# Attention scores from two fp32r halves on quarters of the array, scored closer behind their maxima, with the sums fetched first in each step

## The chip, the cores and the metric

The kernel runs on one core of a Trainium2 chip. The metric is the device time of one execution in microseconds. Five engines work side by side, each through its own list of instructions in order: TensorE (PE) multiplies, VectorE (DVE), ScalarE (ACT) and GpSimd (POOL) work element by element, and SyncE (SP) issues DMAs. They wait for each other through semaphores. A stalled instruction stalls everything behind it on its engine.

## What is computed

A batch of 16 sequences of 512 tokens with 128 features goes through four layers, each with a residual: causal attention, a feed-forward block, rotary attention, and the same feed-forward block again. Both attentions have 16 heads of 8 features.

```python
x = x + attn_a(layernorm(x))   # causal, 3 heads with a reweighted softmax
x = x + ffn(layernorm(x))
x = x + attn_b(layernorm(x))   # rotary positions, no mask
x = x + ffn(layernorm(x))
# attention: q, k, v = x @ W + b
scores = einsum('bhqd,bhkd->bhqk', q, k) / sqrt(8)
out = einsum('bhqk,bhkd->bhqd', softmax(scores), v) @ Wo + bo
# ffn: h = silu(x w1) * (x w2); h = gelu(h h1); h = gelu(h h2); h w3
```

## The kernel before

Everything stays on the chip in `x`; only the stacks described below and the reciprocals of the denominators take a way through DRAM. Each attention stage is a software pipeline over 16 batch entries. In step `n`, batch `n+1` is normalised and projected to q, batch `n` gets its k and v, batch `n-1` gets the row maxima of its scores (`maxes` on PE, `max_of` on DVE), batch `n-2` gets its scores, exponentials (ACT) and weighted sums of v (`weigh` on PE), batch `n-3` has its sums fetched and its denominators inverted, and batch `n-4` is projected out. A step is cut into beats: 20 in the causal stage, 32 in the rotary one. The tables `CAUSAL_AT` and `ROTARY_AT` say in which beat each piece of other work stands, on each engine. In a beat PE multiplies one pair of score tiles for the maxima (M) and one for the scores proper (S), and one or two blocks of weighted sums (W), in the order MSWX or SMWX, X being the other work.

Scores need full precision. Before, q and k are each split on POOL into three bf16 parts (`high`, `middle_low`), SP stores the parts into `d_stack` in DRAM (`store`) so that six products lie under each other, and loads them back as stacks of 48 rows (`load`), one stack for each half of the array's 128 rows. Two more rows of `stack_q` hold the negated maxima in two bf16 parts (`aug`), so that the score product subtracts the maximum by itself. A q stack and a k stack are stored and loaded in every step with a batch.

SP is one list. In a step (`sync`) it issues, in this order: the q load of batch `n`, the x load, the maxima of heads in the second half of batch `n-2` (`aug` 1), the sums and denominators of batch `n-3` (`numerators`), the k store, the reciprocals, the k load, the reciprocals spread to 128 rows, the maxima of the first half of batch `n-1` (`aug` 0), and the q store of batch `n+1`. PE may not start the scores of a half before the `aug` of that half has landed:

```python
if i % (BEATS // 2) == 0:
    h = i // (BEATS // 2)
    pe.wait_ge(s[f"aug{h}"], count(32, b, 32))
```

The causal stage also masks the diagonal twice: for the maxima by small bf16 products of 64 rows (`mask_q`, `ident_s`) right behind each M, and for the exponentials on POOL (`mask`).

## Time and profile before

| | us |
|---|---|
| median of 3 runs | 2139.06 |
| lowest and highest | 2135.49, 2146.88 |
| the profiled execution, its own time | 2145.3 |
| the span of its profile | 2143.6 |

The causal stage takes from about 60 to 600 us of the span, the first feed-forward block to about 1000 us, the rotary stage to about 1740 us, and the second feed-forward block the rest. The rows are read by stage: a step is one trip of the pipeline, and its length is the number of microseconds in a window divided by the steps in it, counted by an instruction that stands a known number of times in each.

### The profile page before, as it was taken

The numbers are of one execution on the slowest core, as the hardware profiler recorded it, in microseconds if no ns is written. First come the engines' busy times: TensorE is split into PE (matmuls) and PEld (weight loads), VectorE is DVE, ScalarE is ACT, GpSimd is POOL, SyncE is SP. The second block draws the span as 40 slices with busy tenths as digits, with TensorE's granted clock in tenths as the row PEclk, the third lists the DMA queues.
The fourth block names the chain that finished last, engine by engine and source line by source line (L and its number), as shares of the span: only waits on it lengthen the run. The fifth ranks groups of instructions, "written<-read, shape, count | busy, mean of one in ns | idle before, by whom it ended". The sixth has DMA issues, their size and how long they took to land.

```text
span 2143.6 us, 43057 instructions
## 1 busy us (share of the span) xinstructions
PE 1941.3 (91%) x16196; PEld 980.7 (46%) x16196; DVE 1719.6 (80%) x2342; ACT 1481.3 (69%) x2641; POOL 1097.3 (51%) x1553
## 2 busy tenths in 40 slices
PE   3789998899879999997899999999999978999998
PEld 1333333334337777774222222222222226777776
DVE  4888887788738888875889999899998936888883
ACT  1477777677766666652588888888887875666665
POOL 5777777677445555564423333434333014555554
PEclk9799999899989999998799999999999999999999
DMA  7456665656210000004344443344444100000000
GB/s 176 95 117 127 118 128 108 111 110 124 49 24 29 1 1 1 1 7 82 61 82 92 92 87 72 72 91 88 92 87 87 33 13 12 15 11 15 11 15 16
DMA packets 106357, 136.71 MB, mean 64 GB/s; under 512 B 21153, under 2 KB 90018, under 8 KB 100002
## 3 DMA queue, kind: packets, MB, share of 16 engines
q1 hardware_dynamic: 106146, 133.89, 31.2%
q8 instruction: 133, 2.18, 0.5%
q14 instruction: 78, 0.64, 0.1%
HBM read 67.78 MB, written 55.58 MB: 58 GB/s over the span
## 4 chain that ended last, share of the span: by engine, by line
PE 48%; POOL 12%; SPq 10%; DMA 10%; issue 9%; DVE 7%; ACT 4%; POOLq 0%; ACTq 0%; DVEq 0%
PE ps_score L1451 20%; PE ps_out L1061 7%; PE ps_max L1451 5%; PE ps_score L1003 5%; SPq L580 4%; DMA o_num<-o_raw 4%; DVE negmax L872 4%; PE ps_max L1021 3%; DMA d_stack<-parts 3%; PE ps_out L1451 3%; ACT prob L989 2%; DMA stack_q<-nm_rows 2%; POOL xhat L322 2%; PE ps_max L1102 2%; SPq L558 2%
## 5 line engine op out<-in xcount | busy, mean ns | idle before, releaser
L989 ACT ACTIVATE prob<-ps_score 128x512 f32<-128x512 f32 x1664 | 899.1, 597 | 209.1 <-PE ps_score L1003 191.0
L872 DVE TENSOR_REDUCE negmax<-ps_max 128x2 f32<-128x1024 f32 (+1 forms) x896 | 907.4, 1064 | 141.0 <-PE ps_max L1038 84.7
L1061 PE MATMUL ps_out<-prob,v_aug 128*9 128x256 f32 (+2 forms) x6656 | 518.9, 392 | 27.4 <-ACT o_raw L952 24.0
L1451 PE MATMUL ps_score<-h,w_hi 128*128 128x512 f32 x2048 | 503.5, 399 | 9.4 <-POOL h L1225 8.3
L1451 PEld LDWEIGHTS ps_score<-h,w_hi 128*128 128x128 f32 x2048 | 383.6, 189 | 104.3 <-POOL h L1225 10.8
L1003 PE MATMUL ps_score<-stack_q,stack_k 50*128 50x512 bf16 (+3 forms) x2048 | 360.3, 353 | 58.0 <-ACT prob L989 38.8
L1021 PE MATMUL ps_max<-stack_k,stack_q 48*128 48x512 bf16 (+3 forms) x2048 | 344.7, 355 | 56.4 <-DVE negmax L872 32.6
L708 POOL TENSOR_SCALAR_AFFINE_SELECT prob<-prob 128x256 f32<-128x256 f32 (+1 forms) x448 | 188.1, 440 | 154.9 <-ACT prob L989 154.6
L1213 POOL TENSOR_TENSOR h<-h3f,h 128x512 fp32r<-128x512 f32 x128 | 192.0, 1508 | 134.0 <-ACT h L1363 134.0
L1003 PEld LDWEIGHTS ps_score<-stack_q,stack_k 50*128 50x128 bf16 x2048 | 105.4, 94 | 313.9 <-ACT prob L989 237.0
L1061 PEld LDWEIGHTS ps_out<-prob,v_aug 128*9 128x9 f32 x6656 | 106.2, 89 | 305.9 <-ACT prob L989 148.6
L1213 POOL TENSOR_TENSOR h<-h2f,h 128x512 fp32r<-128x512 f32 x128 | 172.6, 1350 | 66.7 <-ACT h L1363 66.7
L1021 PEld LDWEIGHTS ps_max<-stack_k,stack_q 48*128 48x128 bf16 x2048 | 87.7, 95 | 217.6 <-DVE negmax L872 103.6
L668 POOL TENSOR_TENSOR qf<-qf,turned 128x512 f32<-128x512 f32 x31 | 39.7, 1280 | 261.6 <-DVE turned L849 261.6
L1357 ACT ACTIVATE h3f<-ps_score,s_col 128x512 f32<-128x512 f32 x128 | 87.5, 684 | 112.3 <-PE ps_score L1451 108.2
L1357 ACT ACTIVATE h2f<-ps_score,s_col 128x512 f32<-128x512 f32 x128 | 88.1, 688 | 95.2 <-PE ps_score L1451 89.1
L1267 DVE CAST h<-h1f 128x512 fp32r<-128x512 f32 x120 | 124.8, 1040 | 35.0 <-PE ps_score L1451 33.9
L1451 PE MATMUL ps_max<-ffn_xT,w_hi 128*128 128x512 f32 x512 | 144.7, 415 | 3.2 <-DVE ffn_xT L1274 2.5
L332 DVE TENSOR_SCALAR xhat<-x,mv,rstd 128x128 f32<-128x128 f32 x128 | 95.1, 803 | 44.1 <-POOL rstd L304 44.1
L1254 DVE SCALAR_TENSOR_TENSOR ut<-tanh,ps_max 128x512 f32<-128x512 f32 x128 | 86.8, 678 | 54.2 <-ACT tanh L1374 51.6
L1269 DVE TENSOR_TENSOR h<-h1f,h 128x512 fp32r<-128x512 f32 x120 | 115.3, 961 | 4.1
L1102 PE MATMUL ps_max<-xT,weights 128*128 128x512 f32 x176 | 107.4, 694 | 4.0 <-ACT xT L933 3.0
(114 smaller groups left out, 2104.2 us busy)
## 6 DMA issues: line engine op xcount, KB each, us to landing
d_stack<-parts SPq DMA_DIRECT2D x128, 192.0 KB, 2.8
stack_q<-d_stack SPq DMA_DIRECT2D x64, 384.0 KB, 6.0
stack_k<-d_stack SPq DMA_DIRECT2D x64, 384.0 KB, 6.0
d_stack<-parts SPq DMA_DIRECT2D x128, 128.0 KB, 2.8
d_stack<-parts SPq DMA_DIRECT2D x128, 64.0 KB, 2.4
o_num<-o_raw SPq DMA_DIRECT2D x128, 64.0 KB
o_rden<-d_rden SPq DMA_DIRECT2D x128, 64.0 KB
x<-in_x SPq DMA_DIRECT2D x16, 256.0 KB, 6.9
```

The costliest lines, as they stand in the source:

```text
L708: last = pool.affine_select(out=tri, in_=tri, compare_op=ALU.is_ge, fill=0.0, base=0, pattern=[[0, tri.shape[1]], [1, P]], channel_multipl ...
L872: last = dve.tensor_reduce(m["negmax"][:, t, :, p], banks[:, :, at:at + w], AX.X, ALU.max, negate=True)
L989: act.activation(prob(b, i)[:, o], act_bank("score", 2 * i + o), ACT.Exp).then_inc(s["prob"], 1)
L1003: mm = pe.matmul(act_bank("score", 2 * i + o)[:, at:at + w], m["stack_k"][c][rows, p, P * j:P * (j + 1)], m["stack_q"][c][rows, p, S - w:S ...
L1021: last = pe.matmul(to[:, o, at:at + w], m["stack_q"][c][rows, p, P * t:P * (t + 1)], m["stack_k"][c][rows, p, 0:w], start=(piece == 0), st ...
L1061: last = pe.matmul(m["ps_out"][32 * g:32 * g + HD + 1, out:out + w], m["v_aug"][b % VALUES][:, j, 4 * G + g, :], prob(b, beat)[:, g % 2, l ...
L1102: pe.matmul(to, m["weights"][:, which], m["xT"][:], start=True, stop=True).then_inc(s[f"{name}_ps"], 1)
L1213: pool.tensor_tensor(h[k][:, 1, f], hf[k][:, f % 2], h[k][:, 0, f], ALU.subtract).then_inc(s[f"h{k}"], 1)
L1267: dve.tensor_copy(h[1][:, 0, f], h1f[:, f % 2]).then_inc(s["h1_hi"], 1)
L1269: dve.tensor_tensor(h[1][:, 1, f], h1f[:, f % 2], h[1][:, 0, f], ALU.subtract).then_inc(s["h1"], 1)
L1357: act.activation(hf[k][:, f % 2], m["ps_hid"][:, f % 2], ACT.Gelu, scale=m["s_col"][:, k, f:f + 1]).then_inc(s[f"h{k}f"], 1)
L1451: mm = pe.matmul(to, w[:, cols], moving(part), start=begin and i == 0, stop=last and i == len(pairs) - 1)
```

## The change

1. The q and k stacks are made of two fp32r parts and three products instead of three bf16 parts and six. POOL makes them with two instructions (`halves`) in place of four. A stack for a group of four heads now lies in a quarter of the array's rows: 24 rows from each multiple of 32, and the negated maximum in one more. `d_stack` is fp32 with the product index outside the quarter index. A load is four DMAs of 24 rows, a store is two DMAs of 128 rows.
2. The maxima need no split: PE transposes them in fp32, POOL's two instructions for them are gone, and `aug` is one DMA in place of two.
3. A pair `p` of heads lies in rows of quarters `2*(p%2)` and `2*(p%2)+1`, so a product pair takes two quarters, and M beats take the odd pair first. The mask products stay 64 rows high.
4. Scores, exponentials and sums of a batch stand `ahead` beats earlier: 4 in the causal and 7 in the rotary stage. Several slots in the tables move with them.
5. In a step SP issues the `numerators` first, ahead of the q load.
6. The flag of the weights' low part is moved in the last causal step.

```diff
-TERMS = 6
+TERMS = 3
 KROWS = TERMS * HD
-AUG = 2
+QUAD = P // 4
-LOADS = 2 * 16
+LOADS = 4 * 16
...
-CAUSAL_AT = {"k": 3, "nm1": 1, "v": 5, "proj": 8, "xT": 9, "nm0": 13, "q": 13, "weigh": (4, 5, 6, 7, 7), "out": 8,
+CAUSAL_AT = {"k": 3, "nm1": 2, "v": 5, "proj": 8, "xT": 9, "nm0": 12, "q": 13, "P_norm": 7, "P_v": 4, "P_bias": 11, "P_q1": 16, "P_k1": 4,
...
+             "D_proj": 9, "A_nm1": 3, "A_nm0": 13, "A_xT": 10, "order": "MSWX", "ahead": 4}
...
-    m["d_stack"] = dram("d_stack", (2, 2, 2, TERMS, HD, PAIRS, S), BF16)
+    m["d_stack"] = dram("d_stack", (2, 2, TERMS, 4, HD, GROUPS, S), F32)
...
     def aug(sp, h, b):
 
         sp.wait_ge(s[f"nm_row{h}"], b + 1)
-        for o in range(2):
-            at = SIDE * o + KROWS
-            sp.dma_start(m["stack_q"][b % STACKS][at:at + AUG, HALF * h:HALF * (h + 1), :],
-                         m["nm_rows"][2 * HALF * o:2 * HALF * (o + 1), h, :]).then_inc(s[f"aug{h}"], 16)
+        sp.dma_start(m["stack_q"][b % STACKS][KROWS::QUAD, GROUPS // 2 * h:GROUPS // 2 * (h + 1), :].bitcast(F32),
+                     m["nm_rows"][QUAD * h:QUAD * h + H // 2].bitcast(F32)).then_inc(s[f"aug{h}"], 16)
...
     def store(sp, b, name, i):
...
+        rows = m["d_stack"][b % 2, i].rearrange("t o d g n -> (o d g) t n")
+        parts = m["parts"][:, i].bitcast(F32)
+        if i == 0:
+            sp.dma_start(rows[:, 0:2], parts[:, 0:1].broadcast_to([P, 2, S])).then_inc(s[name], 16)
+            sp.dma_start(rows[:, 2:3], parts[:, 1:2]).then_inc(s[name], 16)
...
     def load(sp, b, name, stored, i):
...
-        for o in range(2):
-            rows = slice(SIDE * o, SIDE * o + KROWS)
-            sp.dma_start(m[name][b % STACKS][rows], m["d_stack"][b % 2, i, o].rearrange("t d p n -> (t d) p n"))\
-                .then_inc(s[name], 16)
+        for o in range(4):
+            rows = slice(QUAD * o, QUAD * o + KROWS)
+            sp.dma_start(m[name][b % STACKS][rows].bitcast(F32), m["d_stack"][b % 2, i, :, o]).then_inc(s[f"{name}{b % 2}"], 16)
...
     def sync(sp, n):
 
+        if on(n, 3):
+            numerators(sp, n - 3)
         if n == 0:
             store(sp, n, "stored_k", 1)
         if on(n, 0):
             load(sp, n, "stack_q", "stored_q", 0)
         if causal and on(n, -X_AHEAD):
             load_x(sp, m, a, n + X_AHEAD)
         if on(n, 2):
             aug(sp, 1, n - 2)
-        if on(n, 3):
-            numerators(sp, n - 3)
...
-    def high(pool, b, name, i):
+    def halves(eng, b, name, i):
...
+        eng.tensor_copy(m["parts"][:, i, 0], m["qf"][:, i]).then_inc(s["highs"], 1)
+        eng.wait_ge(s["highs"], count(2, b, i + 1))
+        wait(eng, s["parts"], count(2, b, i))
+        eng.tensor_tensor(m["parts"][:, i, 1], m["qf"][:, i], m["parts"][:, i, 0], ALU.subtract).then_inc(s["parts"], 1)
...
-    def scores(pe, n, i):
+    def scores(pe, n, b, i):
...
+                at_row = QUAD * (2 * (p % 2) + o)
+                rows = slice(at_row, at_row + KROWS + 1)
```

In the source of a load the three products lie 65,536 elements apart and the eight features of a product 2,048 apart, so the DMA reads it as 3 runs of 8 rows of 8 KB and writes it to 24 rows. Before, source and target were both plainly 48 rows.

SP's list in one causal step, before, from the q load on (sizes are partitions x elements of the target):

```order
L592 DMA stack_q<-d_stack 48x4096 [waits a_stored_q,a_score]
L592 DMA stack_q<-d_stack 48x4096
L548 DMA stack_q<-nm_rows 2x4x512 [waits a_nm_row1]
L548 DMA stack_q<-nm_rows 2x4x512
L555 DMA den<-o_raw 128x1x64 [waits a_rden,a_o_raw]
L558 DMA o_num<-o_raw 32x1x512 [waits a_oT]
```

and the same stretch of SP's list now, with the k load that follows it:

```order
L553 DMA den<-o_raw 128x1x64 [waits a_rden,a_o_raw]
L556 DMA o_num<-o_raw 32x1x512 [waits a_oT]
L556 DMA o_num<-o_raw 32x1x512 x3
L592 DMA stack_q<-d_stack 24x1x2048 [waits a_stored_q,a_score]
L592 DMA stack_q<-d_stack 24x1x2048 x3
L546 DMA stack_q<-nm_rows 4x2x512 [waits a_nm_row1]
L579 DMA d_stack<-parts 128x2x512 [waits a_parts]
L580 DMA d_stack<-parts 128x512
L561 DMA d_rden<-rden 128x64 [waits a_rden]
L592 DMA stack_k<-d_stack 24x1x2048 [waits a_stored_k,a_score]
L592 DMA stack_k<-d_stack 24x1x2048 x3
```

The sums (`o_num`) moved ahead of the q load, the q load became four DMAs, and the maxima row of the second half still stands right behind it.

PE's list in the causal stage where the second half of the scores begins, before:

```order
L1021 MATMUL ps_max<-stack_k,stack_q 128x128 [waits a_resid]
L1021 MATMUL ps_max<-stack_k,stack_q 128x128
L1021 MATMUL ps_max<-stack_k,stack_q 128x384 x2
L1038 MATMUL ps_max<-ident_s,mask_q 128x2x64 x4
L1003 MATMUL ps_score<-stack_q,stack_k 128x512 [waits a_prob,a_aug1]
L1003 MATMUL ps_score<-stack_q,stack_k 128x512 [waits a_prob]
```

and now:

```order
L979 MATMUL ps_max<-stack_k,stack_q 128x256 [waits a_k]
L979 MATMUL ps_max<-stack_k,stack_q 128x256 x3
L996 MATMUL ps_max<-ident_s,mask_q 128x2x64 x4
L1060 MATMUL ps_max<-weights,xT 128x128 [waits a_xT,a_max]
L1060 MATMUL ps_max<-weights,xT 128x128 x3
L960 MATMUL ps_score<-stack_q,stack_k 128x512 [waits a_prob,a_aug1]
L960 MATMUL ps_score<-stack_q,stack_k 128x512 [waits a_prob]
L979 MATMUL ps_max<-stack_k,stack_q 128x128 [waits a_max]
```

The wait for `aug1` stood in beat 10 of a causal step and stands in beat 6 now; in the rotary stage it moved from beat 16 to beat 9. That for `aug0` moved from beat 0 of the next step to beat 16 (causal) and 25 (rotary) of the step before.

## Rows read from the trace of the kernel before

**Rows 1.** Page, part 1: busy time and share of the span.

```profile
PE 1941.3 (91%) x16196; PEld 980.7 (46%) x16196; DVE 1719.6 (80%) x2342; ACT 1481.3 (69%) x2641; POOL 1097.3 (51%) x1553
```

**Rows 2.** Windows of causal and rotary stages: length, busy by engine, clock, DMA, GB/s.

```profile
100.00:550.00 450.00, 400.73 (x5218) 172.23 (x5212) 368.00 (x524) 330.65 (x626) 325.15 (x656) 0.95 0.61 118
...
1100.00:1600.00 500.00, 470.81 (x4568) 133.66 (x4570) 454.52 (x501) 418.56 (x785) 176.44 (x262) 1.00 0.42 83
```

**Rows 3.** Groups of instructions, causal window 100 to 550 us: busy, mean | idle before.

```profile
L868 DVE TENSOR_REDUCE negmax<-ps_max 128x4 f32<-128x1024 f32 x52 | 63.3, 1218 | 12.7 <-PE ps_max L1038 12.1
...
L708 POOL TENSOR_SCALAR_AFFINE_SELECT prob<-prob 128x256 f32<-128x256 f32 x313 | 121.5, 407 | 95.7 <-ACT prob L989 95.7
```

**Rows 4.** Chain of waits, causal stage: start, length, what.

```profile
302.10 0.42 SPq L592
...
305.41 0.68 SPq L548
306.13 3.88 DMA stack_q<-nm_rows
310.06 0.39 PE ps_score L1003 x2
...
390.53 11.65 DMA o_num<-o_raw
```

**Rows 5.** Timeline of SP, causal stage: start, length, DMAs issued.

```profile
315.86 0.78 SPq L592 DMA_DIRECT2D stack_q<-d_stack  x2
...
319.29 3.15 SPq L558 DMA_DIRECT2D o_num<-o_raw  x4
```

**Rows 6.** Windows of 1 us, columns as in rows 2; the last two are DMA.

```profile
1304.00:1305.00 1.00, 1.00 (x7) 0.32 (x3) 0.76 (x1) 0.87 (x2) 0.00 (x0) 1.00 0.96 206
...
1313.00:1314.00 1.00, 1.00 (x12) 0.14 (x12) 1.00 (x2) 0.95 (x3) 0.92 (x2) 1.00 0.44 161
...
1326.00:1327.00 1.00, 1.00 (x14) 0.26 (x12) 1.00 (x2) 0.74 (x2) 0.29 (x1) 1.00 0.96 172
...
1329.00:1330.00 1.00, 1.00 (x16) 0.28 (x12) 1.00 (x2) 1.00 (x3) 0.90 (x1) 1.00 0.54 131
```

**Rows 7.** Page, part 6: DMA issues, KB each, median us from issue to landing.

```profile
stack_q<-d_stack SPq DMA_DIRECT2D x64, 384.0 KB, 6.0
```

**Rows 8.** Timeline of PE in causal beats at either clock: start, length, instruction.

```profile
407.15 1.04 PE L1061 MATMUL ps_out<-prob,v_aug 128*9 128x256 f32 x8
...
415.35 0.62 PE L1061 MATMUL ps_out<-prob,v_aug 128*9 128x256 f32 x8
415.90 0.39 PE L1021 MATMUL ps_max<-stack_k,stack_q 48*128 48x512 bf16 x2
416.13 0.22 PE L1038 MATMUL ps_max<-ident_s,mask_q 64*128 64x64 bf16 x4
416.19 0.38 PE L1003 MATMUL ps_score<-stack_q,stack_k 50*128 50x512 bf16 x2
416.50 0.83 PE L1061 MATMUL ps_out<-prob,v_aug 128*9 128x384 f32 x8
```

**Rows 9.** Window behind a long causal stall, columns as in rows 2.

```profile
402.00:412.00 10.00, 8.58 (x87) 3.21 (x89) 4.20 (x5) 6.53 (x13) 3.87 (x8) 0.62 0.37 77
```

**Rows 10.** Waits in the rotary window 1100 to 1600 us: total, times, longest.

```profile
DVE negmax L872 <- PE ps_max L1021: 29.4, 46, 1.4
...
PE ps_out L1061 <- ACT o_raw L952: 18.7, 22, 1.7
```

**Rows 11.** Timeline of SP, rotary stage: start, length, DMAs issued.

```profile
1277.13 0.78 SPq L592 DMA_DIRECT2D stack_q<-d_stack  x2
...
1307.13 0.78 SPq L592 DMA_DIRECT2D stack_k<-d_stack  x2
...
1322.54 0.78 SPq L592 DMA_DIRECT2D stack_q<-d_stack  x2
```

More of the change, by code:

```diff
@@ L154, in buffers @@
         low("oT_pad", [P, S])
-        m["stack_q"] = [stack_q] + [low(f"stack_q{c}", [P, PAIRS, S], BF16) for c in range(1, STACKS)]
+        m["stack_q"] = [stack_q] + [low(f"stack_q{c}", [P, GROUPS, S], F32R) for c in range(1, STACKS)]
     h1, h2 = (sb(f"h{k}", [P, 2, FT, S], F32R) for k in (1, 2))
@@ L374, in __init__ @@
-        self.group = len(per_group)
-        self.beats = GROUPS * self.group
-        self.steps = B + 4
-        self.rotary = not causal
-        self.scores = [[(2 * G + half, j, at, w) for half, j, at, w in pieces] for G in range(GROUPS) for pieces in per_group]
-        self.diagonals = diagonals * GROUPS
-        self.maxes = [[(2 * G + half, t, at, w) for half, t, at, w in pieces] for G in range(GROUPS) for pieces in maxes]
-        self.weigh_at, self.reads, self.weighed = [], [], []
-        for G in range(GROUPS):
-            for at, beats, products in blocks:
-                self.weigh_at.append(self.group * G + at)
-                self.reads.append(self.group * G + beats[-1])
-                self.weighed.append((G, [(j, out, w, [(self.group * G + beat, lo) for beat, lo in where])
-                                         for j, out, w, where in products]))
@@ L395, in block_due @@
+        self.beats, self.blocks = len(self.scores), len(blocks)
+        self.weigh_at = [block[0] for block in blocks]
+        self.reads = [block[2] for block in blocks]
+        self.weighed = [(block[1], block[3:]) for block in blocks]
+        self.block_of = {beat: i for i, block in enumerate(blocks) for beat in block[6]}
     def block_due(self, i):
@@ L440, in attention @@
     for i in range(BEATS):
-        act_turns += [("score", 2, 2 * i + o) for o in range(2)]
+        step, at = ahead(0, i)
+        act_turns += [("score", 2 - step, 2 * at + o) for o in range(2)]
         dve_turns += [("max", 1, i)]
@@ L1042, in weigh @@
     def weigh(pe, b, k):
-        G, products = plan.weighed[k]
+        G, (j, out, w, beats, lo, start) = plan.weighed[k]
         first = k % (BLOCKS // GROUPS) == 0
```

303 lines of the change are left out of this document (134 added, 169 removed).

## The prediction

> **What bounds the kernel now.** I read the shares first, then the windows by stage, then the waits and the chain in each stage. No engine fills the span, PE comes nearest with 91% [rows 1], and the attention stages are where the change works.
>
> Causal stage: `L868` stands four times in a step and 52 times in 450 us [rows 3], so there were 13 steps of 34.6 us. PE was busy 400.73 us, 30.8 a step, and DVE 28.3 [rows 2]: nobody is full. The chain shows what is late. SP issues loads and stores one after another, and the small DMA with the maxima waits behind the k load and takes 3.88 us before PE may score; elsewhere ACT waits 11.65 us for `o_num`, queued the same way [rows 4]. The step is a loop through POOL, SP and the DMA queue.
>
> Rotary stage: a q load is issued at 1277.13 and at 1322.54 [rows 11], so a step is 45.4 us. DVE is busy 454.52 of 500 us, 41.3 a step, PE 42.8 [rows 2]. DVE sets the pace and loses 29.4 us in 500 to PE; PE loses 18.7 us to ACT's `o_raw` at the start of batches [rows 10]. At most 4.1 us a step are there to be won.
>
> **POOL and SP work.** Two of POOL's four split instructions per stack go and two copies and subtractions for maxima. POOL is busy 325.15 of 450 us in the causal stage [rows 2] and sits in its loop. SP's six store issues become two and the two of `aug` one, at 0.6 to 0.7 us each, against two loads more at 0.42 us [rows 4]. That would take some 4 us of issue time off the causal loop. It pays only if nothing else is late.
>
> **Sums first.** `o_num` no longer queues behind the q load, so the 11.65 us waits of the causal stage [rows 4] and the 18.7 us of the rotary one, 1.7 a step [rows 10], go. The price is that the q load is issued after them. In a causal step (t counts from PE's first beat) `o_num` waits for POOL's `weighted` of beat 1, about t = 3.9; its four issues take 3.15 us [rows 5]; the q load's issues start at 7.0 and its data at about 8.2.
>
> **PE.** M and S stay pairs of two products at a time, 512 columns in 0.23 us and S in 0.31 with what follows [rows 8]. In the causal stage M and S stand in different quarters, but four mask products of 64 rows lie between them; in the rotary stage both fall in the same half of the array (S is seven beats ahead and M starts with the odd pair), so nothing runs four wide in a beat. From M to mask, both on 64 rows, PE needs 0.23 us for 0.21 us of columns; from S to W, where the array is cut differently, 0.31 [rows 8]. So a new cut costs about 0.09 us. Going to the mask's 64 rows and back to 32 adds two in each causal beat: 20 x 2 x 0.09 = 3.6 us, and the fp32 transposes of the maxima 0.4. PE would have 34.8 us a causal step, 1.75 a beat. TensorEngine Tiling (Array Packing), section Key Properties, of the Trainium skill says that a change of tiling mode drains TensorE; by a reading in which the 32 and 64 row cuts count as one mode the 3.6 us would be 0. The trace before has no such change, so the bounds are 0 and 3.6 us, and I take 3.6, the price of the nearest one. Narrow products of 128 columns may cost more in fp32r: from nothing to 2.6 us a step, four times their columns (16 x 0.16 us). I take nothing and keep 2.6 for the range.
>
> **The load, on which I stake the forecast.** What a DMA spreads over follows the outermost size of its two sides. Stores with 64 rows on both sides fill 0.96 of the 16 DMA engines [rows 6] (the window from 1304). `o_rden` and `o_num` have 8 on their DRAM or source side and 32 on the other, and while four of them are queued the share stays at 0.44 and 0.54, that is, 7 to 9 engines [rows 6] (from 1313 and 1329). Four queued DMAs would fill 16 if each took other engines; they take the same eight. The new load has 3 outermost on one side and 24 on the other, so I expect three engines, and the four DMAs of a stack one behind another on the same three. The Trainium skill's DMA: Bandwidth & Descriptors, section "Why a DMA increments its semaphore by 16 and not by 1", says the same: the largest number up to 16 that divides both slowest dims, and on this path the lowest-numbered engines.
>
> A stack is still 786 KB: 262 KB for each of the three. Per engine the load before moved 172 / (16 x 0.96) = 11.2 GB/s, eight engines 161 / (16 x 0.44) = 22.9 GB/s [rows 6] (from 1326 and 1313). So the load occupies the three for L = 23.4 us or 11.4 us, where before it landed in 6.0 [rows 7]. I take 11.4: the rate per engine doubled where fewer worked.
>
> What stands behind it is the same `aug`, which now takes four engines, the three among them, and is needed sooner.
>
> - Causal: `aug` 1 lands at 8.2 + 11.4 + 2.5 (x load and its own landing) = 22.1. PE wants it in beat 6, t = 10.5. PE, and with it everyone, stands 11.6 us. 14 beats are left, 24.5 us, and PE comes back at a low clock: behind a stall like that the granted clock was 0.62 over 10 us [rows 9], its lower level of 1.2 GHz for much of it, and a W took 1.04 us in place of 0.62 [rows 8]; I put 2.5 us on it. Step: 49.1 us.
> - The other chain of the same step: the k store (48 KB an engine at 206 / (16 x 0.96) = 13.4 GB/s, 3.6 us [rows 6]) lands 4.8 us after `aug` 1, the k load starts 1 us later and takes 11.4, `o_rden` 1.4, `aug` 0 0.8. That is t = 41.5 for PE's beat 16, and 48.5 for the step. I take 49: 14.4 us more than 34.6.
> - Rotary: data from t = 5.7, `aug` 1 lands at 5.7 + 11.4 + 0.9 = 18.0. PE wants it in beat 9, at 1.42 us a beat t = 12.8. PE loses 5.2 us, which DVE feels but for a beat that it gets back as fewer waits of the old kind (1.5), against 1.5 for the clock. Step: 50.6, 5.2 more. `aug` 0 lands at about 39, before beat 25.
>
> The sum, against the profiled execution's 2145.3 us. 14 steps in each stage have a q load and a batch to score: 14 x 14.4 = 202 and 14 x 5.2 = 73. The first batch's two loads are longer by 7 us each with nothing to hide them in the causal stage, 14, and half hidden by the feed-forward block in the rotary one, 7. The stages' tails are 4 and 7 beats of exponentials shorter, 1.2 us each: -13. Total 2145.3 + 283 = 2428. The median stands 6 us under the profiled execution, so **about 2422 us**.
>
> **Rivals.**
> 1. *The load spreads over 16 engines after all* (each DMA on other engines, or cut otherwise). Then every wait above is gone and the step is PE's: causal 31.6 us without the 3.6, -42, rotary -21, tails -13: about 2065 us. With the 3.6 it is causal +8: about 2115. For it: the bytes are the same, the pieces of a store are 2 KB instead of 1. Against: the shares of four queued DMAs [rows 6]. It decides at L below 6 us, where `aug` 1 is in time again. Chance 0.10.
> 2. *Three engines, but at 11.2 GB/s each*, the rate of the old load. L = 23.4, and both stages follow the long chain: causal 18.8 + 2 L + 7 = 72.6 us, rotary 61.4 + 10 = 71.4. 14 x 38 + 14 x 26 + 57 - 13 = 940: about 3080 us. For it: that load read DRAM as this one does, `o_rden` reads it too but in little. Against: sixteen engines shared what three now have. Chance 0.08.
> 3. *Three engines, but most of the wait is covered*: SP runs ahead of my times, POOL's `weighted` comes earlier, or an engine moves more than 23 GB/s. At half the added wait 2290 us, at a quarter 2215; at less it is no change. Chance 0.10, of which 0.03 within 0.5%.
>
> **How the numbers follow.** The forecast has 0.72. L from 9 to 16 us, the cuts of the array at 0 or 3.6 us and the narrow products at 0 or 2.6 us a causal step give 2340 to 2640. With the third rival's greater part the range is 2250 to 2640: it leaves out the first rival, the second, and the far end of the third. A measurement of this kernel tells 0.5%, some 11 us, from no change. Faster 0.10 (rival 1), same 0.03, slower 0.87.
>
> **What would show it.** Right: in windows of a microsecond within a load the DMA share is near 3/16 = 0.19, and loads land in 10 us or more instead of 6; PE's longest waits are for `stack_q<-nm_rows`, some 10 us a causal step in beat 6, and the granted clock of the causal stage falls well under 0.95; the feed-forward stages are as before. Of the smaller steps: PE's time from M to the mask products grows from 0.23 to 0.32 us, and ACT no longer waits for `o_num` by 11 us. Wrong: a DMA share above 0.9 in a load. If the share is 0.19 and the steps are still short, my times of issue are wrong; if the loads take over 16 us, the rate per engine is.

## The result and the profile after

| | before | after |
|---|---|---|
| median, us | 2139.96 | 2662.18 |
| lowest and highest | 2135.49, 2146.88 | 2626.93, 2683.82 |
| the profiled execution, its span | 2145.3, 2143.6 | 2664.05, 2662.3 |

The changed kernel takes 1.238 times as long (95% interval 1.226 to 1.251). The forecast was 2422 us, with a range of 2250 to 2640: the sign holds, the size doesn't.

The page of the changed kernel, busy time and share of the span, then PE's granted clock in 40 slices. It answers to [rows 1].

```profile
PE 2317.5 (87%) x16196; PEld 1185.9 (45%) x16196; DVE 1748.7 (66%) x2340; ACT 1493.6 (56%) x2641; POOL 972.5 (37%) x1297
...
PEclk6678888788767999996858685866768688799999
```

PE has as many instructions as before and is busy 376 us more. The clock is low in both attention stages (slices 1 to 13 and 19 to 35), and full in the feed-forward stages. As in [rows 2], the windows of both attention stages: length, busy by engine, clock, DMA, GB/s.

```profile
150.00:600.00 450.00, 328.12 (x3824) 150.36 (x3818) 273.75 (x385) 245.76 (x461) 204.80 (x409) 0.83 0.27 86
1350.00:1750.00 400.00, 379.76 (x2526) 131.77 (x2524) 264.27 (x276) 234.33 (x435) 73.35 (x96) 0.72 0.18 58
```

The causal stage waits (PE busy 73%). The rotary stage does not: PE is busy 95% of the time, at 0.72 of its clock. The same two windows, groups by line: the reductions of the maxima, of which four (L826) make a causal step and 32 (L830) a rotary one.

```profile
L826 DVE TENSOR_REDUCE negmax<-ps_max 128x4 f32<-128x1024 f32 x38 | 45.9, 1208 | 0.2
...
L830 DVE TENSOR_REDUCE negmax<-ps_max 128x2 f32<-128x1024 f32 x193 | 234.9, 1222 | 104.3 <-PE ps_max L979 103.9
```

38/4 = 9.5 causal steps in 450 us are 47.4 us each (34.6 before). 193/32 rotary steps in 400 us are 66.3 us each; the kernel before has this row with x279 in a window of 400 us inside the stage, 45.9 us.

The whole difference can be laid out by the first and the last product for maxima of each stage. PE's timeline has them at these times (start, length, instruction):

```profile
46.95 0.90 PE L979 MATMUL ps_max<-stack_k,stack_q 24*128 24x128 f32 x4 [19.47 <-issue]
...
790.13 0.50 PE L979 MATMUL ps_max<-stack_k,stack_q 24*128 24x512 f32 x2
...
1198.82 0.80 PE L979 MATMUL ps_max<-stack_k,stack_q 24*128 24x512 f32 x4 [8.20 <-DMA stack_k<-d_stack]
...
2239.34 0.41 PE L979 MATMUL ps_max<-stack_k,stack_q 24*128 24x512 f32 x2
```

In the kernel before the same four stand at 42.96, 582.80, 984.55 and 1722.79. So the causal stage grew from 539.8 to 743.2 us (**+203**), the rotary one from 738.2 to 1040.5 (**+302**), and fill, first feed-forward block and last block by 4 + 7 + 2. The table uses these two lengths for every kernel, each from its profiled execution. Those lie within 6 us of the medians, but for f3 (30 us longer) and e2 (27 us shorter).

| kernel | median, us | ratio to before, 95% | causal | rotary |
|---|---|---|---|---|
| before | 2139.96 | | 539.8 | 738.2 |
| changed | 2662.18 | 1.226 to 1.251 | 743.2 | 1040.5 |
| e1 loads on 8 engines | 2332.98 | 1.085 to 1.093 | 665.4 | 805.4 |
| e2 loads on 12 | 2338.50 | 1.084 to 1.102 | 648.6 | 802.3 |
| e3 before, loads on 3 | 2381.80 | 1.109 to 1.114 | 648.1 | 842.1 |
| e4 maxima before q load | 2443.11 | 1.139 to 1.147 | 746.2 | 811.1 |
| f1 bf16 | 2531.16 | 1.163 to 1.175 | 687.7 | 970.6 |
| f2 8 engines, SP's old order | 2601.56 | 1.207 to 1.223 | 657.6 | 1070.8 |
| f3 8 engines, maxima first | 2581.79 | 1.191 to 1.208 | 647.1 | 1090.8 |
| f4 before, sums first | 2123.44 | 0.986 to 0.994 | 527.4 | 730.1 |
| g1 fp32r on halves | 2491.46 | 1.159 to 1.167 | 731.9 | 888.5 |
| g2 bf16 on halves | 2424.14 | 1.128 to 1.136 | 697.2 | 856.2 |
| h1 8 engines; sums, maxima, load | 2253.92 | 1.049 to 1.056 | 592.7 | 803.3 |
| h2 before; sums, maxima, load | 2118.29 | 0.986 to 0.992 | 528.7 | 725.6 |
| i1 h1, bf16 | 2179.44 | 1.015 to 1.023 | 566.9 | 756.4 |
| i2 h1, fp32r on halves | 2222.06 | 1.036 to 1.044 | 566.6 | 798.8 |
| i3 h1, bf16 on halves | 2161.94 | 1.008 to 1.015 | 555.9 | 754.5 |

**The causal stage took the time that was forecast.** The chain of waits of the changed kernel in one causal step (start, length, what) is the one that the forecast wrote down; it answers to [rows 4].

```profile
315.37 1.25 POOL oT L679
316.64 0.71 SPq L556
...
320.00 0.73 SPq L592
...
323.64 11.31 DMA stack_q<-nm_rows
334.99 0.48 PE ps_score L960
```

POOL's product of beat 1, the four `o_num`, the q load, and then a small DMA that lands 11.31 us after its issue because it stands behind the load. PE's waits there, total, times, longest, in 150 to 600 us:

```profile
PE ps_score L960 <- DMA stack_q<-nm_rows: 105.1, 9, 12.5
...
ACT o_raw L908 <- DMA o_num<-o_raw: 14.0, 8, 2.1
```

105.1/9 = 11.7 us a step; the forecast had 11.6. ACT's long wait for `o_num` is gone, as it had said. And in a microsecond in the middle of a load the DMA share is near 3/16, against the 0.96 of a load before in [rows 6] (from 1326):

```profile
1338.00:1339.00 1.00, 1.00 (x16) 0.41 (x12) 1.00 (x2) 0.88 (x2) 0.97 (x1) 1.00 0.17 74
```

**The rotary stage did not.** PE's waits for the maxima in 1350 to 1750 us:

```profile
PE ps_score L960 <- DMA stack_q<-nm_rows: 14.3, 4, 3.8
```

That is 2.4 us a step, where the forecast had 5.2. The wait is shorter than forecast; what follows it is longer. PE's timeline at full clock, and behind a wait:

```profile
1301.14 0.50 PE L960 MATMUL ps_score<-stack_q,stack_k 25*128 25x512 f32 x2
1301.48 0.41 PE L979 MATMUL ps_max<-stack_k,stack_q 24*128 24x512 f32 x2
...
1302.36 0.52 PE L960 MATMUL ps_score<-stack_q,stack_k 25*128 25x512 f32 x2
...
1342.79 0.79 PE L960 MATMUL ps_score<-stack_q,stack_k 25*128 25x512 f32 x2 [3.50 <-DMA stack_q<-nm_rows]
...
1344.91 0.79 PE L960 MATMUL ps_score<-stack_q,stack_k 25*128 25x512 f32 x2
```

A beat takes 1.22 us at full clock and 2.12 us behind the wait of 3.50 us. Windows of 5 us, of which many are left out, show how long that lasts (the clock is the third number from the end):

```profile
1335.00:1340.00 5.00, 4.29 (x36) 1.28 (x34) 4.36 (x5) 3.26 (x6) 2.16 (x3) 1.00 0.21 87
1340.00:1345.00 5.00, 2.21 (x14) 0.72 (x14) 1.25 (x2) 1.08 (x2) 0.99 (x1) 0.60 0.52 193
1345.00:1350.00 5.00, 5.00 (x28) 1.65 (x28) 2.72 (x3) 2.17 (x4) 0.00 (x0) 0.50 0.16 59
...
1415.00:1420.00 5.00, 5.00 (x23) 1.59 (x19) 2.36 (x3) 1.16 (x3) 0.00 (x0) 0.55 0.00 0
1420.00:1425.00 5.00, 5.00 (x54) 1.75 (x56) 4.91 (x6) 4.38 (x9) 3.17 (x3) 1.00 0.13 50
```

For 75 us PE is busy nearly all the time, at 1.2 GHz, and then goes back to 2.4. Between 1300 and 1800 us there are five such stretches: 80, 50, 20, 80 and 50 us. The Trainium skill, TensorE: Matmul & The Clock Gate, section "Part 1: The HAM clock gate", has PE at full clock again after a short time of sustained work. Behind this wait it took 75 us of it, and the measurement decides.

### The profile page after: what moved, and what is told of

It reads as the page before. It is cut to its first block, busy times and chain, and to the rows that moved or that the text cites. A ratio compares the mean times of both kernels' runs of the same rounds, so it can differ in the third digit from the quotient of the medians.

```text
span 2662.3 us, 42605 instructions
## 1 busy us (share of the span) xinstructions
PE 2317.5 (87%) x16196; PEld 1185.9 (45%) x16196; DVE 1748.7 (66%) x2340; ACT 1493.6 (56%) x2641; POOL 972.5 (37%) x1297
## 4 chain that ended last, share of the span: by engine, by line
PE 68%; DMA 12%; issue 7%; SPq 4%; ACT 3%; POOL 3%; DVE 2%; POOLq 0%; ACTq 0%; DVEq 0%
PE ps_out L1017 17%; PE ps_score L1409 16%; PE ps_score L960 12%; DMA stack_q<-nm_rows 10%; PE ps_max L979 6%; PE ps_max L1409 4%; PE ps_max L1057 3%; SPq L592 3%; ACT prob L945 2%; PE ps_out L1409 2%; PE ps_max L996 2%; PE ps_max L1087 2%; PE ps_score L1027 1%; DMA d_stack<-parts 1%; SPq L556 1%
## 5 line engine op out<-in xcount | busy, mean ns | idle before, releaser
L830 DVE TENSOR_REDUCE negmax<-ps_max 128x2 f32<-128x1024 f32 (+2 forms) x896 | 937.2, 1068 | 559.4 <-PE ps_max L996 280.2
L960 PE MATMUL ps_score<-stack_q,stack_k 25*128 25x512 f32 (+3 forms) x2048 | 525.6, 520 | 237.9 <-DMA stack_q<-nm_rows 202.7
L1017 PE MATMUL ps_out<-prob,v_aug 128*9 128x256 f32 (+2 forms) x6656 | 635.0, 469 | 15.1 <-ACT o_raw L908 11.7
L960 PEld LDWEIGHTS ps_score<-stack_q,stack_k 25*128 25x128 f32 x2048 | 221.9, 216 | 695.6 <-ACT prob L945 332.4
L979 PE MATMUL ps_max<-stack_k,stack_q 24*128 24x512 f32 (+3 forms) x2048 | 451.9, 468 | 46.3 <-issue 19.5
L979 PEld LDWEIGHTS ps_max<-stack_k,stack_q 24*128 24x128 f32 x2048 | 224.1, 229 | 68.8 <-issue 33.9
L1222 DVE CAST h<-h1f 128x512 fp32r<-128x512 f32 x120 | 125.3, 1044 | 34.8 <-PE ps_score L1409 33.7
L1057 PE MATMUL ps_max<-xT,weights 128*128 128x512 f32 x176 | 123.7, 792 | 3.8 <-ACT xT L889 3.0
```

Of the source, the lines that this page charges most:

```text
L830: last = dve.tensor_reduce(m["negmax"][:, t, p // HALF, side:side + 2, p // 2 % 2], banks[:, :, at:at + w], AX.X, ALU.max, negate=True)
L960: mm = pe.matmul(act_bank("score", 2 * i + o)[:, at:at + w], m["stack_k"][c][rows, p // 2, P * j:P * (j + 1)], m["stack_q"][c][rows, p // ...
L979: last = pe.matmul(to[:, o, at:at + w], m["stack_q"][c][rows, p // 2, P * t:P * (t + 1)], m["stack_k"][c][rows, p // 2, 0:w], start=(piece ...
L1017: last = pe.matmul(m["ps_out"][32 * g:32 * g + HD + 1, out:out + w], m["v_aug"][b % VALUES][:, j, 4 * G + g, :], prob(b, beats[g // 2])[:, ...
L1057: pe.matmul(to, m["weights"][:, which], m["xT"][:], start=True, stop=True).then_inc(s[f"{name}_ps"], 1)
L1222: dve.tensor_copy(h[1][:, 0, f], h1f[:, f % 2]).then_inc(s["h1_hi"], 1)
```

## Experiments

My theory behind the result had three parts: the loads on three engines make the maxima late (A); behind the wait PE stays at 1.2 GHz, on quarters far longer than on halves (C1); and the fp32r products cost PE about 0.1 us a beat at full clock (D1). The rivals were that the products and not the loads are the cause (B), that the type keeps the clock down (A1, C2), and that the cut into quarters makes the products dear (A2, D2).

### e1 and e2: loads on more engines

e1 only lays the rows of a load in another order; e2 also changes `d_stack` and stores in three DMAs.

```diff
-            sp.dma_start(m[name][b % STACKS][rows].bitcast(F32), m["d_stack"][b % 2, i, :, o]).then_inc(s[f"{name}{b % 2}"], 16)
+            sp.dma_start(m[name][b % STACKS][rows].bitcast(F32), m["d_stack"][b % 2, i, :, o].rearrange("t d g n -> d t g n")).then_inc(s[f"{name}{b % 2}"], 16)
```

```diff
-    m["d_stack"] = dram("d_stack", (2, 2, TERMS, 4, HD, GROUPS, S), F32)
+    m["d_stack"] = dram("d_stack", (2, 2, 4, HD, TERMS, GROUPS, S), F32)
```

> The changed kernel with one line altered: a load lays its 24 rows in the order feature, product instead of product, feature, so its source has 8 outermost in place of 3. Stores, products and SP's order stay. Theory A (three engines make the load 10 us long, the maxima row behind it is late, PE stalls, and behind the stall its clock stays at 1.2 GHz for long): DMA share in a load 0.5, a load of four DMAs in 4 to 6 us, PE's waits for stack_q<-nm_rows under 1 us a step, granted clock over 0.95 in both stages. The time is then PE's own: rotary 32 beats of about 1.25 us and its other work, 47 us a step; causal 32 to 35 us; whole kernel 2110 to 2220 us. Theory B (the products on quarters, not the load, are what costs, and they pull the clock down): over 2400 us, the clock in the rotary stage still about 0.7.

> The changed kernel with the stack in DRAM laid so that the 24 rows of a quarter follow each other (24 outermost on both sides), and a store in three DMAs of 128 rows in place of two. If the engines of a DMA are the largest number up to 16 that divides both outermost sizes, this is 12 engines: DMA share 0.75 in a load, load 4 to 5 us. Theory A: within 2% of the kernel with 8 engines, 2110 to 2220 us, since both are in time for the maxima row. If more engines still bring more (theory: the long chain of store, load and maxima sets the causal step), it is 30 us or more below the one with 8. Theory B: over 2400 us.

2332.98 and 2338.50 us. One line takes 329 of the 522 us away, so A holds for that much, and B, which wanted over 2400 us, falls. In e1's load the windows of 1 us read:

```profile
376.00:377.00 1.00, 0.00 (x0) 0.00 (x0) 0.54 (x5) 1.00 (x3) 0.00 (x0) 1.00 0.47 172
```

Half of 16 engines and about twice the bytes a second of three (the 74 GB/s above). e2's four runs spread from 2311 to 2358 us, so that twelve engines bring nothing that can be told from eight. In e2 the windows of the load rise over 0.7, with other DMAs beside it. The rule in DMA: Bandwidth & Descriptors of the Trainium skill, section "Why a DMA increments its semaphore by 16 and not by 1", gives 3, 8 and 12 engines for these three loads; the shares 0.17 and 0.47 agree for the first two.

But both kernels miss what I expected by over 110 us. The rotary stage is at clock 1.00 with 261/32 steps in 400 us, 49.0 us, as expected. The causal stage took 42.9 us a step and not 32 to 35, for PE still waits for the maxima:

```profile
PE ps_score L960 <- DMA stack_q<-nm_rows: 79.4, 11, 8.0
```

7.2 us a step. SP's timeline in one of them:

```profile
368.99 3.27 SPq L556 DMA_DIRECT2D o_num<-o_raw  x4
372.36 3.47 SPq L592 DMA_DIRECT2D stack_q<-d_stack  x4
...
376.36 0.59 SPq L546 DMA_DIRECT2D stack_q<-nm_rows  x1
```

The issues alone take 7.4 us from POOL's product to the small DMA, which lands 6.01 us later. It is wanted in beat 6. Even a fast load is late if it stands between.

### e3: the kernel before with slow loads

The load of the kernel before with 3 outermost, in four DMAs. `d_stack`, the view that a store writes and the semaphores of the loads follow from it; nothing else changes.

```diff
-    m["d_stack"] = dram("d_stack", (2, 2, 2, TERMS, HD, PAIRS, S), BF16)
+    m["d_stack"] = dram("d_stack", (2, 2, TERMS, 2, HD, PAIRS, S), BF16)
...
-            sp.dma_start(m[name][b % STACKS][rows], m["d_stack"][b % 2, i, o].rearrange("t d p n -> (t d) p n"))\
-                .then_inc(s[name], 16)
+            for t in range(0, TERMS, 3):
+                rows = slice(SIDE * o + HD * t, SIDE * o + HD * (t + 3))
+                sp.dma_start(m[name][b % STACKS][rows], m["d_stack"][b % 2, i, t:t + 3, o]).then_inc(s[f"{name}{b % 2}"], 16)
```

> The kernel before with nothing of the change but the load: the product index outside the half index in DRAM, and four DMAs of 24 rows with 3 outermost in a load. bf16, halves of the array, SP's order and the beats of the scores stay. Theory A: DMA share 0.19 in a load and 10 to 11 us for a load. In the rotary stage the maxima rows are wanted in beat 16 and at the end of the step, so nothing waits: 45 to 46 us a step and clock 1.0. In the causal stage the two loads stand in SP's loop: 34.6 us and 4 to 9 us more a step. Whole kernel 2200 to 2280 us. Rival (a slow load costs the same wherever the maxima are wanted): over 2450 us, with the clock of the rotary stage under 0.8.

2381.80 us: slow loads by themselves cost 242 us, 108 in the causal stage, 104 in the rotary one, and the rest while the stages fill. The causal half was expected; in the rotary stage I had said that nothing waits. It does: `aug` 0, behind the k load, is wanted at the start of the next step, and PE waits 48.9 us in 7 times in 400, at most 8.0. What follows such a wait is the finding:

```profile
1440.00:1445.00 5.00, 0.74 (x4) 0.21 (x4) 0.00 (x0) 0.04 (x1) 1.24 (x2) 0.50 0.67 168
1445.00:1450.00 5.00, 5.00 (x36) 0.76 (x36) 3.24 (x3) 3.22 (x6) 0.43 (x3) 0.55 0.11 33
1450.00:1455.00 5.00, 5.00 (x50) 1.42 (x50) 4.40 (x5) 4.33 (x9) 0.00 (x0) 1.00 0.19 80
```

Behind 8 us of standstill this kernel is at full clock again within 6 us; the changed one took 75 behind 3.5.

### e4: the same slow loads, without the wait in the rotary stage

```diff
         if on(n, 3):
             numerators(sp, n - 3)
+        if on(n, 2):
+            aug(sp, 1, n - 2)
...
         if causal and on(n, -X_AHEAD):
             load_x(sp, m, a, n + X_AHEAD)
-        if on(n, 2):
-            aug(sp, 1, n - 2)
```

> The changed kernel with the maxima of the second half (aug 1) issued by SP ahead of the q load instead of behind it; the load stays on three engines. Theory A: PE's wait in causal beat 6 and rotary beat 9 is gone. The other chain stays (q load 10 us, k store, k load 10 us, then the maxima of the first half): it lands at about 41 us of a causal step where PE wants it at 28, so causal stays at 45 to 48 us; in the rotary stage it lands at 38 to 40 us against 36, so a short wait may be left; if it is there the clock falls with it, if not a rotary step is 47 to 50 us at a clock over 0.95. Whole kernel 2350 to 2560 us. Rival (the clock falls without a stall, from the products themselves): rotary clock still 0.7 with PE's waits for the maxima under 1 us a step.

2443.11 us. All of the gain of 219 us is in the rotary stage (1040.5 to 811.1); the causal stage stays, as expected, since its other chain is as long. The window of the rotary stage:

```profile
1300.00:1800.00 500.00, 482.00 (x4277) 179.36 (x4276) 443.06 (x467) 392.09 (x736) 123.06 (x161) 1.00 0.24 79
```

The same products on the same quarters, PE busy 96%, and clock 1.00 for 500 us. The products by themselves do not pull the clock down. With PE's wait gone the low clock is gone, and behind a wait the same products take long to bring it back.

### f2 and f3: eight engines in other orders

f2 is e1 with SP's order of before (load, maxima, sums):

```diff
-        if on(n, 3):
-            numerators(sp, n - 3)
...
         if on(n, 2):
             aug(sp, 1, n - 2)
+        if on(n, 3):
+            numerators(sp, n - 3)
```

f3 is e1 with maxima, sums, load:

```diff
+        if on(n, 2):
+            aug(sp, 1, n - 2)
         if on(n, 3):
             numerators(sp, n - 3)
...
-        if on(n, 2):
-            aug(sp, 1, n - 2)
```

> The kernel with loads on eight engines, and SP's order of the kernel before: q load, x load, maxima of the second half, and only then sums (part 5 of the change undone). In e1 the chain in a causal step was POOL's product of beat 1, four o_num issues of 3.3 us, the q load's four of 3.5, and 6 us until the maxima land, while PE stands 7.4 us. Theory A: with the q load no longer behind o_num that wait is under 2 us; causal step 43 to 35-38 us; ACT waits again for o_num, up to 5 us a step; the rotary step stays at 49 us since PE's products set it. Whole kernel 2220 to 2270 us. Rival (the causal step is set by the long chain of loads and stores and not by this wait): within 1% of 2333 us.

> The kernel with loads on eight engines, and in each step the maxima of the second half ahead of sums and q load (maxima, sums, q load). Theory A: the wait of 7.4 us in causal beat 6 goes; q load, k store, k load and the maxima of the first half follow later than in f2, landing near 28 to 31 us of a step where PE wants them at 28, so causal 35 to 39 us, and rotary 49. Whole kernel 2220 to 2290 us, within 1% of f2. Rival as for f2: within 1% of 2333 us.

2601.56 and 2581.79 us, the two largest misses: some 300 us over what I expected, and 11% slower than e1. The maxima are in time now, but the sums are late. PE's timeline of f2:

```profile
1365.02 1.04 PE L1017 MATMUL ps_out<-prob,v_aug 128*9 128x256 f32 x8 [6.41 <-ACT o_raw L908]
```

ACT waits for `o_num` before it may overwrite `o_raw`, PE waits 6.41 us for ACT, and the clock stays at 1.2 GHz from there on. The causal stage even gained 8 and 18 us against e1; the rotary one lost 265 and 285. In f3 sums and maxima both stand ahead of the load, and PE waits as long. SP's timeline there, and PE's:

```profile
1426.17 0.58 SPq L546 DMA_DIRECT2D stack_q<-nm_rows  x1
...
1427.79 3.26 SPq L556 DMA_DIRECT2D o_num<-o_raw  x4
```

```profile
1435.06 1.04 PE L1017 MATMUL ps_out<-prob,v_aug 128*9 128x256 f32 x8 [6.78 <-ACT o_raw L908]
```

SP stands at the maxima until ACT has written their row, and the sums stand behind them. In e1, where the sums come first, PE's longest wait for ACT in the rotary stage was 0.5 us. So with this kernel's rotary table (its scores seven beats ahead) the sums must go first of all; that the maxima go ahead of the load matters too, with slow loads (e4) and in the causal stage (e1).

### f1, g1, g2: what keeps the clock down

f1 takes the upper bf16 half of each word, and leaves out the lower one. g1 reads halves of the array, so that each product sums two groups of heads. g2 does both. Loads and SP's order are those of the changed kernel. The first edit is f1's, the second one of g1's two; g1 also clears the rows between the stacks.

```diff
+    def top(words):
+        return words.bitcast(BF16)[:, 1::2]
```

```diff
-                at_row = QUAD * (2 * (p % 2) + o)
-                rows = slice(at_row, at_row + KROWS)
+                rows = slice(SIDE * o, SIDE * o + QUAD + KROWS)
```

> The changed kernel, loads still on three engines, with every product of M and S made from the upper bf16 half of each fp32 word (a strided view) in place of the fp32r word; rows, quarters, columns, DMAs, waits and order stay. What is left out: the lower half of the words, so scores are coarser. Theory A1 (the fp32r products are what costs: 0.11 us more per pair, and PE, kept at 1.2 GHz with no time to spare behind a stall, stays there): M and S pairs 0.23 us at full clock as before, the low clock ends within 10 us of a stall of 4 to 12 us, rotary step 48 to 53 us in place of 66, causal about as now (45 to 48, set by the landing of the maxima), whole kernel 2400 to 2490 us. Theory A2 (it is the cut into quarters, whatever the type): pairs stay at 0.33 us, the low clock lasts 20 to 90 us, 2600 to 2670 us.

> The changed kernel, loads on three engines and all waits in place, with M and S reading halves of the array: 56 and 57 rows from 0 or 64 in place of 24 and 25 from a quarter. Still fp32r. What differs in the result: each product sums two groups of heads. Three memsets per stage are added so that the rows between the stacks are defined. Question: what keeps PE at 1.2 GHz behind a stall for 60 to 90 us in the rotary stage, when the kernel before with slow loads (bf16, halves, e3) is back after 5 to 10 us? Theory C1 (the products on quarters): with halves it is back within 10 us of a stall, rotary step 50 to 56 us, whole kernel 2430 to 2520 us. Theory C2 (fp32r, or the tables of this kernel): it stays low as before, 62 to 67 us a step, 2600 to 2690 us. From S to M 0.33 us at full clock as on quarters, since with bf16 on quarters (f1) it was 0.24.

> As g1, and the products from the upper bf16 half of each word, as in f1: halves and bf16 together, with the tables, waits and slow loads of the changed kernel. Theory C1: back at full clock within 10 us of a stall, rotary step 48 to 53 us, whole kernel 2380 to 2450 us. Theory C2, if fp32r is it: the same here, and g1 over 2600. If the tables are it: a rotary step of 60 us or more here too, 2530 us or more (f1, bf16 on quarters, took 2531).

2531.16, 2491.46 and 2424.14 us. f1 lies between what A1 (the type) and A2 (the quarters) expected, and neither holds alone: its pairs take 0.24 us at full clock, as A1 said, and its clock stays low for up to 55 us, as A2 said. g1 and g2 came as C1 expected. I counted, in windows of 5 us, the stretches that begin between 1300 and 1800 and in which the granted clock is under 0.75:

| rotary stage, slow loads | stretches, us | rotary length |
|---|---|---|
| changed: fp32r, quarters | 80, 50, 20, 80, 50 | 1040.5 |
| f1: bf16, quarters | 50, 20, 20, 15, 20, 55, 20, 50 | 970.6 |
| g1: fp32r, halves | nine of 5 or 10 | 888.5 |
| g2: bf16, halves | eight of 5 or 10 | 856.2 |
| e3: bf16, halves, tables of before | nine of 5 or 10 | 842.1 |

On halves none of these 26 stretches is over 10 us, with either type and either table; on quarters, in these two kernels, none is under 15, and with fp32r they are longer. The waits ahead of them are no longer on quarters: at most 3.8 us in the changed kernel and 4.8 in f1, against 4.1, 5.2 and 8.0 on halves. f2 and f3 (fp32r, quarters, waits of 6 us) show both kinds: 10, 120, 10, 15, 10, 120 and 85, 5, 10, 10, 10, 115; in each of those over 100 us PE waited a second time. What holds in these windows doesn't hold where a stage fills: g1 and g2 have a stretch of 60 us at the start of theirs, in which PE stands for long; g1 was back some 15 us after it had work without a break. g1 behind a wait of some 4 us:

```profile
1500.00:1505.00 5.00, 4.74 (x26) 1.75 (x28) 2.45 (x2) 2.17 (x4) 0.00 (x0) 0.50 0.43 145
1505.00:1510.00 5.00, 4.74 (x44) 1.32 (x44) 3.67 (x3) 3.76 (x8) 0.00 (x0) 0.86 0.30 107
```

### h1: everything in time

e1 with e4's order of SP.

> The changed kernel with loads on eight engines (e1), and SP's order sums, maxima of the second half, q load (e4). e1 had 7.4 us of wait for the maxima in each causal step, f2 and f3 had waits of 5 to 6 us for o_num, which in the rotary stage took the clock down. Theory A: here both land in time: in the rotary stage no stall over 1 us, clock 1.00, 49 us a step; in the causal stage 36 to 39 us, the rest of its length being the chain of two loads and two stores. Whole kernel 2190 to 2250 us, the best of the fp32r kernels, still slower than before by PE's own time: 3.1 us more in a rotary step. Rival (the maxima still late, from their own copy on ACT or the numerators ahead of them): 2300 us or more.

2253.92 us, a hair over the expected range, with no stall over 0.5 us in the rotary stage and 37.5 us a causal step.

### i1, i2, i3: the products at full clock

h1 with f1's, g1's and g2's products, by the same edits.

> The kernel of h1 (loads on eight engines; sums, maxima, load) with the products of M and S from the upper bf16 half of each word, on quarters. What is left out: the lower halves. h1 has hardly a stall, so this prices the products by themselves. Theory D1 (the type costs: behind a pair of 512 columns PE takes 0.33 us in fp32r and 0.24 in bf16, 32 times a rotary step): rotary step 49.0 to 46 us, causal 37.5 to 35.5-36.5, whole kernel 2160 to 2200 us. Theory D2 (the cut into quarters costs): rotary stays over 48 us, 2220 us or more.

> The kernel of h1 with fp32r products on halves, 56 and 57 rows. What differs in the result: each product sums two groups of heads. Theory D1: rotary 49 us as h1. In the causal stage the mask products of 64 rows no longer stand between products of 32-row cuts, and M and S no longer run side by side in different quarters: the two about cancel, 36 to 39 us; whole kernel 2220 to 2290 us. If the change of the cut is the larger (the 3.6 us a step of the forecast), causal 34 to 35.5 us and 2200 us or less.

> The kernel of h1 with the products from the upper bf16 halves on halves of the array: PE's products as in the kernel before, all the rest (loads in four DMAs, two splits on POOL, one copy of the maxima, scores ahead, SP's order) as in the changed kernel. What differs in the result: sums of two groups, and coarse. Theory D1: rotary 46 us, DVE's pace; causal 33 to 35 us; 2120 to 2160 us, which says that what the change saves on POOL and SP is worth 0 to 20 us once nothing stalls. If it is worth more (5 us of issue time and POOL's 2 us off each causal step): under 2100 us.

2179.44, 2222.06 and 2161.94 us, the last 2 us over its range. In the rotary stage the type costs 47 us on quarters and 44 on halves, the cut 2 to 5: D1 holds. PE's timeline of i1 (S, then M) against 1301.14 and 1301.48 above:

```profile
1501.20 0.40 PE L964 MATMUL ps_score<-stack_q,stack_k 25*128 25x512 bf16 x2
1501.44 0.39 PE L983 MATMUL ps_max<-stack_k,stack_q 24*128 24x512 bf16 x2
```

0.24 us in bf16, 0.34 in fp32r. 32 x 0.10 = 3.2 us a step, and h1's step is 49.0 us where the one before was 45.9. The weight loads suggest why; groups of the causal window in e1 (fp32r) and i1 (bf16), mean ns of one behind the busy time:

```profile
L979 PEld LDWEIGHTS ps_max<-stack_k,stack_q 24*128 24x128 f32 x652 | 56.6, 201 | 0.8 <-DVE negmax L830 0.8
```

```profile
L983 PEld LDWEIGHTS ps_max<-stack_k,stack_q 24*128 24x128 bf16 x794 | 27.3, 95 | 2.3 <-DVE negmax L830 2.0 <-DVE negmax L826 0.4
```

Loading 24 rows of 128 weights takes twice as long in fp32r as in bf16; i2 has 187 ns on 56 rows. TensorE: Matmul & The Clock Gate of the Trainium skill, section "Weight-path perf modes — Fast Weight Load (FWL) and DoubleRow", has the fast load on for 128 weights that aren't FP32; the two rows, which the trace calls f32 and bf16, agree with it. That the longer load is what shows as 0.10 us is inferred.

In the causal stage the cut gains time in a beat and loses it by the clock. The changed kernel's causal table says `"order": "SMWX"`; the diff ahead of the prediction prints `"MSWX"` there, and that is wrong. S comes first, then M and its mask products, then W. The same beat in the changed kernel (quarters) and in i2 (halves):

```profile
253.12 0.50 PE L960 MATMUL ps_score<-stack_q,stack_k 25*128 25x512 f32 x2
253.13 0.50 PE L979 MATMUL ps_max<-stack_k,stack_q 24*128 24x512 f32 x2
253.56 0.23 PE L996 MATMUL ps_max<-ident_s,mask_q 64*128 64x64 bf16 x4
253.72 0.83 PE L1017 MATMUL ps_out<-prob,v_aug 128*9 128x384 f32 x8
```

```profile
300.65 0.50 PE L964 MATMUL ps_score<-stack_q,stack_k 57*128 57x512 f32 x2
300.99 0.40 PE L982 MATMUL ps_max<-stack_k,stack_q 56*128 56x512 f32 x2
301.23 0.23 PE L999 MATMUL ps_max<-ident_s,mask_q 64*128 64x64 bf16 x4
301.39 0.83 PE L1020 MATMUL ps_out<-prob,v_aug 128*9 128x384 f32 x8
```

On quarters S and M start together and run side by side. From S to W it is 0.60 us, on halves 0.74; in bf16 0.53 (i1) and 0.62 (i3). The kernel before took 0.60 too, from M to W [rows 8]. What the new cut costs by itself can't be read from this, since S runs within the time from M to the mask products.

Still i2's causal stage is 26 us shorter than h1's, and i3's 11 us shorter than i1's (1.6 and 0.7 us a step). The windows of h1 and of i2 show the clock (third number from the end):

```profile
150.00:600.00 450.00, 414.50 (x4805) 187.82 (x4802) 338.35 (x478) 307.75 (x577) 253.94 (x506) 0.88 0.37 106
```

```profile
150.00:600.00 450.00, 421.87 (x4980) 232.53 (x4972) 357.30 (x484) 318.32 (x598) 259.29 (x517) 1.00 0.37 105
```

Counted in windows of 5 us, the granted clock is under 0.75 for 100 of these 450 us in h1 and never in i2, whose waits are shorter (at most 1.8 us for the maxima, 3.1 in h1). In bf16 the waits are alike, at most 3.3 and 3.1 us, and it is 90 us on quarters (i1) against 25 on halves (i3). So C1's difference shows here too.

### f4 and h2: SP's order alone, on the kernel before

f4 moves the sums, h2 the maxima as well:

```diff
     def sync(sp, n):
+        if on(n, 3):
+            numerators(sp, n - 3)
+        if on(n, 2):
+            aug(sp, 1, n - 2)
...
-        if on(n, 2):
-            aug(sp, 1, n - 2)
-        if on(n, 3):
-            numerators(sp, n - 3)
```

> The kernel before with part 5 of the change alone: sums and denominators issued first in a step. The maxima of the second half are then issued some 4 us later, behind o_num, and land at about 17 us of a causal step, where this kernel wants them in beat 10, at 17.5 us; in the rotary stage there is room. ACT's waits for o_num (11.65 us at the longest) should go. Theory: no long stall, causal 33 to 36 us, rotary 45 to 46, whole kernel 2110 to 2170 us. Rival (sums ahead of the load cost a wait wherever the maxima are wanted): causal 38 us or more and over 2190 us.

> The kernel before with SP's order sums, maxima of the second half, q load. f4 (sums first, maxima still behind the q load) took 2123 us against 2141 and PE still waited 20 us in 450 for the maxima. Theory: these waits go, the q load comes 1.4 us later, 2100 to 2130 us. Rival (the causal step is set by the chain of loads and stores, which the later q load lengthens): 2130 to 2150 us.

2123.44 and 2118.29 us: 0.990 (0.986 to 0.994) and 0.989 (0.986 to 0.992) of the kernel before. **h2 is a little faster than both kernels of this case**: by 24 us, 1.1%, against the one before, with two calls of `sync` in another place. Against h2, i3 has PE's products as cheap, fewer instructions on POOL and scores ahead, and is 44 us slower; what of it is due to which part was not tried.

## Why the forecast was wrong

- **Three engines, one behind another: right.** Share 0.17 for 0.19, wait 11.7 us for 11.6. Going back to eight engines gave 329 us.
- **The length of the causal step: in part luck.** It was 47.4 us for 49, but two terms of it were wrong and in part cancel. In windows of 1 us over 150 to 600 us, PE is busy 76 us at 1.2 GHz, 8 a step; at full clock it would take half, so the clock costs 4 us a step (my estimate), where the forecast put 2.5. By the same count PE's work at full clock is (328 - 38)/9.5 = 30.5 us a step, and not 34.8. That the stage grew by 203 us for 202 is luck as well: 14 steps of 12.8 us more are 179, and the rest lies outside these steps.
- **The clock behind a stall in the rotary stage: the step that failed.** The forecast put 1.5 us a step on it, from [rows 9] and [rows 8], a stall in the causal stage of a kernel on halves. In the changed kernel a stall of 3.5 us was followed by 75 us at 1.2 GHz. In windows of 1 us from 1350 to 1750, 222 of PE's 380 busy us lie at that clock, 37 a step; half of it, 18 us, is what the clock costs in place of 1.5 (my estimate). e4, which differs from the changed kernel in one issue of SP, puts stall and clock together at 229 us of this stage, where the forecast had 73. [rows 2] even gave the reason why it would hurt: a PE that has 42.8 us of work in 45.4 at 2.4 GHz has no room at 1.2. The forecast read there that DVE, with 41.3 us, sets the pace.
- **"512 columns in 0.23 us" in fp32r: wrong by 0.10 us.** 3.1 us a rotary step, 44 to 47 us of the stage; the forecast had nothing. In the causal stage 11 to 26 us. It had priced fp32r by its columns alone, though the page of the kernel before has the weight loads of the feed-forward products, beside 95 ns for `L1021` in bf16:

```profile
L1451 PEld LDWEIGHTS ps_score<-h,w_hi 128*128 128x128 f32 x2048 | 383.6, 189 | 104.3 <-POOL h L1225 10.8
```

- **The cut of the array: 3.6 us a causal step that PE did not need.** The forecast took it from an order M, mask, S that the kernel does not have. In its order S, M, mask, W there is one change of the cut more a beat, not two, and S and M run side by side, so that a beat took no longer than before (0.60 us for 0.60). What quarters cost the stage, 0.7 to 1.6 us a step, goes with the clock.
- **Tails 13 us shorter: not seen.** From the last product for maxima to the end 420.8 us before and 423.0 after; between the stages 401.8 and 408.7, the expected 7 us of fill included.
- **The first rival was mispriced too.** It had 2065 to 2115 us with fast loads, "decides at L below 6 us". e1's load is that fast (786 KB at its 172 GB/s are 4.6 us, my estimate) and took 2333 us. With o_num's issues, the load's issues and the landing the maxima take 13.4 us from POOL's product; PE wanted them in beat 6.

Taken apart from the changed kernel back to the one before, the rotary stage's 302 us are 229 for the wait and its clock (e4), 8 between e4 and h1, 47 for the type (i1), 2 for the cut (i3), and 16 that remain between i3 and the kernel before.

Open: why on quarters PE stays at 1.2 GHz for 10 us in one stretch and 85 in another, what of it is due to fewer rows and what to the cut itself, and what i3 loses against h2.

## What to carry to other kernels

Before a DMA's layout changes, work out over how many engines its outermost sizes spread, and look at what small, urgent transfer stands behind it on the same queue; issue it ahead of the load, but behind what needs no wait, since it holds up all that stands behind it (f3). Where PE has no slack at full clock, price a stall by what the clock does behind it in a kernel that uses as many rows of the array, not by its own length. Price fp32r products by their weight loads as well as their columns.

## What the chip showed that I had not expected

- With products on 24 and 25 rows a single stall of 3.5 to 6.8 us was followed by up to 85 us at a granted clock of 0.50 with PE busy (changed kernel, f2, f3); with 56 and 57 rows or 48 and 50, in the middle of the rotary stage, by 5 to 10 us (g1, g2, e3). Without such a stall the same narrow products ran 500 us at 1.00 (e4).
- Eight engines moved 172 GB/s (e1) and three 74 (the changed kernel) in loads with rows of 8 KB: 23 and 27 GB/s for each busy engine (172 / (16 x 0.47), 74 / (16 x 0.17)), where sixteen moved 11 each before [rows 6].
- Weight loads of 24 x 128 took 201 ns in fp32r (e1) and 95 ns in bf16 (i1).
- Products of 512 columns on different quarters started together and took 0.44 us for both pairs up to the mask products, against 0.58 us on halves (changed kernel, i2).
